# Attention over 6250 keys on one core: output transposes a pair later, values in other rounds, a quarter of the block moves on ScalarE's queue

## The chip, the core and the metric

The kernel runs on one core of a Trainium2 chip. TensorE (PE) multiplies matrices into PSUM, VectorE (DVE), ScalarE (ACT) and GpSimd (POOL) work on SBUF and PSUM, and SyncE (SP) issues DMAs; ACT can issue them too. The engines run side by side and wait for each other by semaphores only. The metric is the device time of one execution in microseconds (us); lower is better.

## The reference, cut to what matters

Eight heads of 64 attend from 512 query rows to 6250 keys and values, then comes a transformer block's rest. `e` is 512, `n` is 6250.

```python
q = (M @ Wq.T).reshape(e, h, dh).transpose(1, 0, 2)
k, v = jnp.split(x @ Wkv.T + bkv, 2, axis=-1)
sim = jnp.einsum('hid,hjd->hij', q, k) * dh ** (-0.5)
sim = jnp.where(mask, sim, -1000000000.0)
out = jnp.einsum('hij,hjd->hid', jax.nn.softmax(sim, axis=-1), v)
out = out.transpose(1, 0, 2).reshape(e, h * dh) @ Wo.T + bo
m = layer_norm(out + M)
z = layer_norm(jax.nn.relu(m @ W1.T + b1) @ W2.T + b2 + m)
```

## The kernel before

The keys are taken in 7 chunks of 896 (first, five in a loop, last), each chunk in 4 pairs of heads p = 0 to 3, each pair in 4 rounds t = 0 to 3, one for 128 query rows. `chunk_schedule` writes one list of steps for a chunk; every engine walks the same list and carries out its part of each step, so the list is the order of work on all queues at once. A step is (letter, pair, index); a pair number below 0 is a pair of the chunk before. The steps:

- **S** (L807, L652): PE computes the scores of the round's two heads into two of three PSUM slots (12 matmuls in float32r, three products for precision); DVE adds the mask, takes the running extreme and writes `prob`. The three slots are a ring, and **K** uses one of them too.
- **E** (L533): ACT takes the exponential of one head's `prob`, with its sum. **X** (L665): DVE transposes 32x32 blocks of both heads of a round from `prob` into `st`. X of round t stands in round t + 1.
- **M** (L366): 16 DMAs on SP's queue carry the blocks of two rounds from `st` to their partitions in `pt`. X of an even round waits until the moves of the same half of `st` one pair earlier have landed.
- **W** (L834): PE multiplies values by the moved probabilities, 7 key tiles of 128 for a pair, into the bank `outT`. W of pair p stands in pair p + 2.
- **C** (L547): ACT copies `outT` to `outT_sb`. **F** (L841): PE transposes that into the bank `tp`. **A** (L672): DVE adds `tp` to the accumulator `acc`.
- **V** (L736 with `tail`, L539): PE projects the values of one key tile into `tp`, ACT copies them to `val`. V and F share the one bank `tp`, so each waits until the one before it has been emptied (`tp_free`). V0 to V3 are made in pair 1, V4 to V6 in pair 2.
- **K** (L736 with `slot`), **H** (L500), **L** (L604): the next pair's keys, their high part on ACT, their low part `k_lo` on DVE. S of the next pair waits for `k_lo`. **Z** (L435 to L446, L554): rescaling of sums and `acc` on POOL, a small exponential on ACT. **Jx**, **Jm**, **J**: loads of `x` and mask, and the split of `x` on POOL. **I**: the loads of `wo`, the residual and the first tiles of `w1` and `w2`, 3 MB in all, in the last chunk.
- After the last chunk: **N** (L675, L678) divides by the sums, **G** (L854) transposes, B and **D** (L551, L681) split the result, **Y** (L770) is the output projection. Then layer norm and the feed-forward loop.

The four rounds of pair 2 of a middle chunk, before:

```
S2.0 E V4 E W0.0 W0.1 W0.2 X1.3 M1.1
S2.1 E V5 E W0.3 W0.4 Z1 X2.0
S2.2 E V6 E W0.5 K3 H3 J X2.1 M2.0
S2.3 E W0.6 C0 E L3 F0 X2.2 A0
```

Of the kernel before, what the change touches and what calls it, by code (L numbers as in the profile page):

```python
# [43 lines left out]
def chunk_schedule(first, last):  # L44

    out = []
    if not first:
        out.append(("M", -1, 1))
    if not last:
        out.append(("Jx", 0, 0))

    def weighted(p, kts):
        return [] if first and p < 0 else [("W", p, kt) for kt in kts]

    for p in range(PAIRS):
        w = p - 2
        keys = not (last and p == PAIRS - 1)
        has_w = not (first and w < 0)

        out.append(("S", p, 0))
        if p == 2:
            out.extend([("E", p, (0, 0)), ("V", 0, 4), ("E", p, (0, 1))])
            out.extend(weighted(w, (0, 1, 2)))
        elif p == 1:  # L70
            out.extend([("E", p, (0, 0)), ("E", p, (0, 1))])
            out.extend(weighted(w, (0, 1, 2)))
            out.append(("V", 0, 0))
        else:
            out.extend([("E", p, (0, 0)), ("E", p, (0, 1))])
            out.extend(weighted(w, (0, 1, 2)))
        if not (first and p == 0):
            out.append(("X", p - 1, 3))
            if p > 0:
                out.append(("M", p - 1, 1))  # L80

        out.append(("S", p, 1))
        if p == 2:
            out.extend([("E", p, (1, 0)), ("V", 0, 5), ("E", p, (1, 1))])
            out.extend(weighted(w, (3, 4)))
        elif p == 1:
            out.extend([("E", p, (1, 0)), ("E", p, (1, 1))])
            out.extend(weighted(w, (3, 4, 5)))
            out.append(("V", 0, 1))
        else:  # L90
            out.extend([("E", p, (1, 0)), ("E", p, (1, 1))])
            out.extend(weighted(w, (3, 4, 5)))
        if not (first and p == 0):
            out.append(("Z", p - 1, 0))
        out.append(("X", p, 0))

        out.append(("S", p, 2))
        if p == 2:
            out.extend([("E", p, (2, 0)), ("V", 0, 6), ("E", p, (2, 1))])
            out.extend(weighted(w, (5,)))  # L100
        else:
            out.extend([("E", p, (2, 0)), ("E", p, (2, 1))])
            out.extend(weighted(w, (6,)))
            if has_w:
                out.append(("C", w, 0))
        if keys:
            out.extend([("K", p + 1, 0), ("H", p + 1, 0)])
        if p == 2 and not last:
            out.append(("J", 0, 0))
        if p == 2 and last:  # L110
            out.append(("I", 0, 0))
        out.extend([("X", p, 1), ("M", p, 0)])
        if p == 0 and not last:
            out.append(("Jm", 0, 0))

        out.append(("S", p, 3))
        out.append(("E", p, (3, 0)))
        if p == 2:
            out.extend(weighted(w, (6,)))
            if has_w:  # L120
                out.append(("C", w, 0))
            out.append(("E", p, (3, 1)))
        elif p == 1:
            out.extend([("V", 0, 2), ("E", p, (3, 1)), ("V", 0, 3)])
        else:
            out.append(("E", p, (3, 1)))
        if keys:
            out.append(("L", p + 1, 0))
        if has_w:
            out.append(("F", w, 0))  # L130
        out.append(("X", p, 2))
        if has_w:
            out.append(("A", w, 0))
            if last and w >= 0:
                out.append(("N", w, 0))
        if last and p == PAIRS - 1:
            out.append(("O", 0, 0))
    if last:
        a, b = PAIRS - 2, PAIRS - 1
        out.extend([("X", b, 3), ("M", b, 1), ("Z", b, 0)])  # L140
        out.extend([("G", 0, 0), ("G", 1, 0), ("B", 0, 0), ("D", 0, 0), ("B", 1, 0), ("D", 1, 0)])
        out.extend([*weighted(a, range(KT)), ("C", a, 0), ("Y", 0, 0), ("F", a, 0), ("A", a, 0), ("N", a, 0)])
        out.extend([("Y", 0, 1), ("Y", 0, 2), ("Y", 0, 3), ("G", a, 0), ("B", a, 0), ("D", a, 0)])
        out.extend([*weighted(b, range(KT)), ("C", b, 0), ("Y", 1, 0), ("F", b, 0), ("A", b, 0), ("N", b, 0)])
# [814 lines left out]
```

## Time and profile before

| what | value |
|---|---|
| three runs | 786.58, 787.69, 788.43 us; median 787.69 |
| the profiled execution | 788.94 us, its span 787.1 us |
| busy share of the span | PE 86%, DVE 74%, ACT 47%, POOL 21% |
| TensorE clock granted, mean | 0.932 of full speed |

The profile comes from one execution. Idle time is put down to what ended it. "Starts" below are us from the start of the span. The setup ends at about 30 us, the seven chunks at about 648, and the output projection and feed-forward part take the rest. S of pair 0 of the fourth chunk starts at 287.17.

### The profile page before, as it was taken

How to read it: one execution, taken by the hardware profiler on the slowest of the kernel's cores; microseconds unless marked ns; L12 is line 12 of the kernel's file. 1: busy time of each engine (PE TensorE's matmuls, PEld its weight loads, DVE VectorE, ACT ScalarE, POOL GpSimd, SP SyncE). 2: the span in 40 equal slices, each digit the busy share in tenths (PEclk: the TensorE clock that was granted, in tenths of full speed). 3: DMA queues.
4: the chain of work that ended last, by engine and by line, in shares of the span. 5: the costliest groups of instructions: out<-in, count | busy, mean ns of one | idle time of the engine just before them, and what ended most of it. 6: DMA issues, size and time to landing. Idle time of an engine off the chain costs nothing.

```text
span 787.1 us, 10971 instructions
## 1 busy us (share of the span) xinstructions
PE 674.7 (86%) x3382; PEld 404.6 (51%) x3382; DVE 581.0 (74%) x715; ACT 367.6 (47%) x658; POOL 163.0 (21%) x239
## 2 busy tenths in 40 slices
PE   4888888899888888898898888888898849699995
PEld 3664444544445444554455444554455425478884
DVE  4498898778887799779987898879878771633333
ACT  4355455554545455555554554555544530333332
POOL 2200320023100420023100320033000070421213
PEclk8889999999999999999999999999999969799998
DMA  8067788767787678868787678867777884022321
GB/s 304 1 155 171 161 181 210 190 157 167 174 237 177 146 179 212 198 140 180 175 237 178 154 175 221 195 142 179 168 170 175 267 192 106 28 80 82 105 80 53
DMA packets 52503, 127.95 MB, mean 163 GB/s; under 512 B 15744, under 2 KB 16256, under 8 KB 52224
## 3 DMA queue, kind: packets, MB, share of 16 engines
q1 hardware_dynamic: 52480, 127.67, 66.5%
q8 instruction: 11, 0.18, 0.1%
q14 instruction: 12, 0.10, 0.0%
HBM read 23.80 MB, written 1.05 MB: 32 GB/s over the span
## 4 chain that ended last, share of the span: by engine, by line
PE 64%; SPq 14%; DVE 10%; issue 6%; DMA 3%; ACT 2%; POOL 0%; DVEq 0%; ACTq 0%; POOLq 0%
PE tail L834 18%; PE slot L807 16%; SPq L366 13%; PE tail L736 10%; PE slot L736 7%; PE slot L887 6%; PE slot L895 5%; DVE st L665 3%; DVE prob L652 3%; DMA pt<-st 2%; DVE k_lo L604 1%; DMA wq_raw<-in_wq 1%; PE tail L841 1%; ACT val L539 1%; DVE stats L689 1%
## 5 line engine op out<-in xcount | busy, mean ns | idle before, releaser
L533 ACT ACTIVATE prob<-prob,negmax 128x896 f32<-128x896 f32 x224 | 234.1, 1045 | 274.7 <-DVE negmax L652 274.7
L652 DVE CUSTOM_DVE_ANT_0 prob<-slot,lower,negmax_old 128x896 f32<-128x896 f32 x224 | 248.8, 1148 | 77.5 <-PE slot L807 73.9
L665 DVE STREAM_TRANSPOSE st<-prob 128x1792 f32<-128x1792 f32 x112 | 228.6, 2041 | 19.8 <-DMA pt<-st 19.3
L834 PE MATMUL tail<-pt,val 128*64 128x512 f32 x784 | 209.4, 664 | 0.4 <-DMA pt<-st 0.4
L807 PE MATMUL slot<-k_hi,q_hi 64*128 64x448 f32 x448 | 98.1, 432 | 50.4 <-DVE k_lo L604 39.5
L834 PEld LDWEIGHTS tail<-pt,val 128*64 128x64 f32 x784 | 54.2, 152 | 110.6 <-issue 110.6
L807 PEld LDWEIGHTS slot<-k_hi,q_hi 64*128 64x128 f32 x448 | 44.0, 191 | 106.1 <-issue 63.4
L807 PE MATMUL slot<-k_hi,q_lo 64*128 64x448 f32 x448 | 88.2, 386 | 0.0
L807 PE MATMUL slot<-k_lo,q_hi 64*128 64x448 f32 x448 | 87.3, 382 | 0.0
L441 POOL TENSOR_TENSOR total<-total,alpha 128x8 f32<-128x8 f32 x28 | 5.8, 206 | 249.8 <-ACT alpha L554 249.8
L807 PEld LDWEIGHTS slot<-k_hi,q_lo 64*128 64x128 f32 x448 | 45.9, 198 | 3.5
L416 POOL TENSOR_SCALAR lower<-mask_raw 128x896 bf16<-128x896 uint8 x28 | 27.2, 971 | 91.5 <-DVE negmax L652 79.7
L807 PEld LDWEIGHTS slot<-k_lo,q_hi 64*128 64x128 f32 x448 | 45.2, 195 | 1.5
L736 PE MATMUL tail<-wv_hi,x_hi 128*128 128x512 f32 x98 | 36.4, 453 | 10.3 <-ACT val L539 10.3
L736 PE MATMUL slot<-x_hi,wk_hi 128*128 128x448 f32 x112 | 36.0, 403 | 8.0 <-DVE x_lo L613 8.0
L533 ACT ACTIVATION_READ_ACCUMULATOR prob<-prob,negmax 128x1 f32 x224 | 42.1, 188 | 0.0
L841 PE MATMUL tail<-ident,outT_sb 128*128 128x128 f32 x112 | 18.7, 291 | 19.6 <-ACT outT_sb L547 14.9
L539 ACT COPY val<-tail 128x512 f32<-128x512 f32 x49 | 28.1, 574 | 15.0 <-PE tail L736 15.0
L736 PEld LDWEIGHTS slot<-x_hi,wk_hi 128*128 128x128 f32 x112 | 19.5, 195 | 30.2 <-issue 29.1
L478 POOL TENSOR_TENSOR hid_lo<-hid,hid_hi 128x512 fp32r<-128x512 f32 x16 | 21.2, 1327 | 66.5 <-DVE hid_hi L720 66.5
L720 DVE CAST hid_hi<-hid 128x512 fp32r<-128x512 f32 x16 | 6.8, 428 | 35.9 <-ACT hid L589 35.8
L435 POOL TENSOR_TENSOR drop<-negmax,negmax_old 128x8 f32<-128x8 f32 x28 | 5.7, 203 | 131.5 <-ACT prob L533 131.0
(107 smaller groups left out, 844.1 us busy)
## 6 DMA issues: line engine op xcount, KB each, us to landing
pt<-st SPq DMA_DIRECT2D x896, 112.0 KB, 2.3
w_raw<-in_w SPq DMA_DIRECT2D x32, 256.0 KB, 2.8
x_raw<-in_x SPq DMA_DIRECT2D x6, 896.0 KB, 5.8
mask_raw<-in_mask SPq DMA_DIRECT2D x7, 448.0 KB, 3.9
mt_raw<-in_mt SPq DMA_DIRECT2D x2, 512.0 KB, 8.0
wq_raw<-in_wq SPq DMA_DIRECT2D x2, 512.0 KB, 8.7
wo_raw<-in_wo SPq DMA_DIRECT2D x1, 1024.0 KB, 4.7
m_res<-in_mn SPq DMA_DIRECT2D x1, 1024.0 KB, 6.9
```

The costliest lines, as they stand in the source:

```text
L366: sp.dma_start(pt[LANES * b:LANES * b + LANES, buf, a], st[LANES * a:LANES * a + LANES, i, b]).then_inc(landed[buf], 16)
L416: nc.gpsimd.tensor_scalar(lower[:, t], mask_raw[:, t], -1.0, -BIG, ALU.add, ALU.mult).then_inc(lower_ready, 1)
L533: nc.scalar.activation(unit, unit, ACT.Exp, bias=negmax[:, p, u:u + 1], scale=-1.0, accum_out=psumrow[:, p, u:u + 1]).then_inc(exp_done, 1)
L539: nc.scalar.copy(val[:, i], tp).then_inc(v_copied, 1)
L652: nc.vector.tensor_tensor_reduce(out=prob[:, i % 2, h].rearrange("p (b n) -> p b n", b=2), in0=slot[:, j, :, :HALF], in1=lower[:, i].rearr ...
L665: nc.vector.transpose(st[:, g].rearrange("p b k (t i) -> p k b t i", t=2)[:, :, :, t2], prob[:, i % 2].rearrange("p h (k b i) -> p (h k) b ...
L736: last = nc.tensor.matmul(dst, stationary(a, k), moving(b, k), start=(n == 0), stop=(n == len(terms) - 1))
L807: last = nc.tensor.matmul(slot[:, j, b, :HALF], q2[qa][rows(h), p, P * i:P * i + P], key_half(p, b, kb)[rows(h)], start=(part == 0), stop= ...
L834: last = nc.tensor.matmul(outT[DH * h:DH * h + DH], val[:, i, head(p, h)], moving, start=(i == 0), stop=(i == KT - 1))
L841: last = nc.tensor.transpose(tp[:, P * t:P * t + P], outT_sb[:, P * t:P * t + P], ident[:])
L887: last = nc.tensor.matmul(slot[:, 2, j], w12[a][:, j, k], mT2[b][:, k], start=(i == 0), stop=(i == len(terms) - 1))
L895: last = nc.tensor.matmul(slot[:, t // 2, t % 2], hid2[a][:, j, P * t:P * t + P], w22[b][:, j], start=first and i == 0, stop=last_one and ...
```

## The change

Three things change in the list of steps; the work itself stays the same.

1. F and A of a pair stand one pair later: C of pair p is in round 2 or 3 of pair p + 2 as before, but F and A are in round 1 of pair p + 3, F ahead of W3, A behind S on DVE. A bank waits for what last stood in it in the list (`bank_plan`), so V5 in pair 2 now waits for A.
2. V1 moves from round 1 to round 2 of pair 1, V5 goes between W3 and W4, V4, V6, V2 and V3 keep their places.
3. M issues 12 of its 16 DMAs on SP; the other 4 are a new step B on ACT's queue, a round later (B0 behind round 3's exponentials, B1 behind round 1's of the next pair).

In the last chunk I stands a round later, behind M2.0; in the ending, G0 goes ahead of W of pair 2 and G1 into it. What B was in the ending is now T.

```diff
+ROUNDS = (
+    ('S E0 E1 W0 W1 W2 X M1 R',
+     'S E0 E1 Z F W3 W4 W5 A X B1',
+     'S E0 E1 W6 C K H X M0 Q',
+     'S E0 E1 L X B0'),
+    ('S E0 E1 W0 W1 W2 V0 X M1',
+     'S E0 E1 Z F W3 W4 W5 A X B1',
+     'S E0 E1 W6 C V1 K H X M0',
+     'S E0 V2 E1 V3 L X B0'),
+    ('S E0 V4 E1 W0 W1 W2 X M1',
+     'S E0 E1 Z F W3 V5 W4 A X B1',
+     'S E0 V6 E1 W5 K H X M0 J',
+     'S E0 W6 C E1 L X B0 I'),
+    ('S E0 E1 W0 W1 W2 X M1',
+     'S E0 E1 Z F W3 W4 W5 A X B1',
+     'S E0 E1 W6 C K H X M0',
+     'S E0 E1 L X B0 O'),
+)
...
+                elif kind in "WC":
+                    step = (kind, p - 2, i)
+                elif kind in "FA":
+                    step = (kind, p - 3, i)
...
+        out.extend([("F", 1, 0), ("A", 1, 0), ("N", 1, 0)])
+        out.extend([("X", b, 3), ("M", b, 1), ("B", b, 1), ("Z", b, 0)])
+        out.extend([("G", 0, 0), ("T", 0, 0), ("D", 0, 0)])
+        out.extend([*(("W", a, kt) for kt in range(3)), ("G", 1, 0), ("T", 1, 0), ("D", 1, 0)])
...
-                        for turn in range(QUAD):
+                        for turn in (0, 1, 2):
                             for a in (0, 2, 1, 3):
...
+                    if kind == "B":
+                        buf = move_buf(p, i)
...
+                        act.wait_ge(xposed, written)
+                        for turn in (3,):
+                            for a in (0, 2, 1, 3):
+                                b = (a + turn) % QUAD
+                                act.dma_start(pt[LANES * b:LANES * b + LANES, buf, a],
+                                              st[LANES * a:LANES * a + LANES, i, b]).then_inc(landed[buf], 16)
...
+            def bank_plan(sched):
+
+                plan, last = {}, None
+                for step in sched:
+                    if step[0] in "VF":
+                        plan[step], last = last, step
+                return plan
```

PE's queue in the loop, pair 2, round 1, from behind the scores of the round to the next round's (`ident` marks F, `wv` marks V, `pt,val` marks two of a W's matmuls). Before:

```order
352 L736 MATMUL tail<-wv_hi,x_hi 128x512 [waits v_copied]
353 L736 MATMUL tail<-wv_hi,x_hi 128x512
354 L736 MATMUL tail<-wv_lo,x_hi 128x512 x2
355 L736 MATMUL tail<-wv_hi,x_lo 128x512 x2
356 L834 MATMUL tail<-pt,val 64x512 [waits v_copied]
357 L834 MATMUL tail<-pt,val 64x512
358 L834 MATMUL tail<-pt,val 64x512 [waits v_copied]
359 L834 MATMUL tail<-pt,val 64x512
360 L807 MATMUL slot<-k_hi,q_hi 128x448 [waits drained2,drained1]
```

And after the change:

```order
351 L821 MATMUL tail<-ident,outT_sb 128x128 [waits outT_copied,v_copied]
352 L821 MATMUL tail<-ident,outT_sb 128x128 x3
353 L814 MATMUL tail<-pt,val 64x512 [waits v_copied]
354 L814 MATMUL tail<-pt,val 64x512
355 L714 MATMUL tail<-wv_hi,x_hi 128x512 [waits acc_added]
356 L714 MATMUL tail<-wv_hi,x_hi 128x512
357 L714 MATMUL tail<-wv_lo,x_hi 128x512 x2
358 L714 MATMUL tail<-wv_hi,x_lo 128x512 x2
359 L814 MATMUL tail<-pt,val 64x512 [waits v_copied]
360 L814 MATMUL tail<-pt,val 64x512
361 L787 MATMUL slot<-k_hi,q_hi 128x448 [waits drained2,drained1]
```

F has come into the round, and V5 waits for `acc_added`, DVE's A, where it waited for a copy of ACT.

DVE's queue of the same round, after the change (L630 is S, L650 is A, L643 is X; before, no A stood between the second S and X):

```order
170 L630 ISA prob,negmax<-slot,lower,negmax_old 128x896 [waits filled2,xposed,zeroed]
171 L630 ISA negmax 128x1
172 L228 REGISTER_ALU
173 L630 ISA prob,negmax<-slot,lower,negmax_old 128x896 [waits filled0,zeroed]
174 L630 ISA negmax 128x1
175 L650 TENSOR_TENSOR acc<-acc,tail 128x512 [waits f_filled,acc_scaled]
176 L642 ISA [waits landed2]
177 L643 STREAM_TRANSPOSE st<-prob 128x14x4x32 [waits exp_done]
```

A stands behind both scores of its round.

ACT's queue from the last exponential of round 0 of pair 0 to the first of round 2, before and after the change:

```order
67 L531 REGISTER_ALU
68 L533 ACTIVATE prob,psumrow<-prob,negmax 128x896 [waits drained0]
69 L554 ACTIVATE alpha<-drop 128x8 [waits drop_ready]
70 L533 ACTIVATE prob,psumrow<-prob,negmax 128x896 [waits drained1]
71 L533 ACTIVATE prob,psumrow<-prob,negmax 128x896 [waits drained2]
```

```order
81 L496 REGISTER_ALU
82 L498 ACTIVATE prob,psumrow<-prob,negmax 128x896 [waits drained0]
83 L532 ACTIVATE alpha<-drop 128x8 [waits drop_ready]
84 L228 ISA
85 L528 DMA pt<-st 32x896 [waits xposed,pv_done,zeroed]
86 L528 DMA pt<-st 32x896 x3
87 L498 ACTIVATE prob,psumrow<-prob,negmax 128x896 [waits drained1]
88 L498 ACTIVATE prob,psumrow<-prob,negmax 128x896 [waits drained2]
```

Four DMAs now stand ahead of the next round's exponentials.

## Rows read from the trace of the kernel before

**Rows 1.** The page's part 4: the chain that ended last, by engine.

```profile
PE 64%; SPq 14%; DVE 10%; issue 6%; DMA 3%; ACT 2%; POOL 0%; DVEq 0%; ACTq 0%; POOLq 0%
```

**Rows 2.** Busy time by stretch: pairs 0 to 3 of the fourth chunk, then three slower pairs.

```profile
core 0: us, PE busy (x) PEld busy (x) DVE busy (x) ACT busy (x) POOL busy (x), PEclk, DMA share, GB/s
287.17:307.18 20.01, 17.07 (x92) 8.92 (x92) 18.33 (x22) 10.32 (x20) 1.82 (x5) 0.91 0.79 176
307.18:332.94 25.76, 23.57 (x116) 13.10 (x116) 20.42 (x23) 12.58 (x24) 2.23 (x7) 0.93 0.88 222
332.94:355.43 22.49, 20.38 (x113) 11.63 (x112) 16.76 (x22) 11.36 (x21) 6.22 (x5) 1.00 0.65 145
355.43:375.45 20.02, 17.08 (x94) 8.94 (x93) 18.13 (x23) 10.70 (x21) 6.47 (x10) 0.91 0.80 180
...
109.30:129.88 20.58, 17.23 (x92) 8.98 (x92) 18.52 (x23) 10.41 (x21) 1.90 (x6) 0.92 0.78 176
178.07:198.60 20.53, 17.15 (x95) 9.00 (x94) 18.10 (x22) 10.65 (x21) 6.42 (x10) 0.92 0.74 166
549.95:570.60 20.65, 17.19 (x92) 9.01 (x92) 18.32 (x22) 10.29 (x20) 1.95 (x6) 0.92 0.75 170
```

**Rows 3.** The chain in order of time, pair 0 into pair 1, two chunks: start, us, what.

```profile
302.25 1.42 PE slot L807 x11
...
306.06 0.01 DVE negmax L652
306.06 1.07 DVE k_lo L604
307.14 0.04 issue
307.18 1.49 PE slot L807 x12
308.68 4.40 PE tail L834 x12
313.08 1.59 PE tail L736 x6
...
397.02 2.73 PE tail L834 x12
```

**Rows 4.** Timeline at pair starts: start, us, engine, line, operation, idle before.

```profile
303.59 0.66 PE L841 MATMUL tail<-ident,outT_sb 128*128 128x128 f32 x4
307.18 0.47 PE L807 MATMUL slot<-k_hi,q_hi 64*128 64x448 f32 x2 [2.94 <-DVE k_lo L604]
...
329.95 0.73 PE L736 MATMUL tail<-wv_hi,x_hi 128*128 128x512 f32 x2 [1.44 <-ACT val L539]
...
332.36 0.66 PE L841 MATMUL tail<-ident,outT_sb 128*128 128x128 f32 x4 [0.75 <-ACT val L539]
...
354.87 0.63 PE L841 MATMUL tail<-ident,outT_sb 128*128 128x128 f32 x4 [2.11 <-ACT outT_sb L547]
```

**Rows 5.** Two starts of pair 1 by stretch, columns as in rows 2.

```profile
395.53:401.20 5.67, 5.67 (x30) 2.86 (x30) 5.39 (x7) 1.72 (x4) 0.40 (x2) 1.00 0.94 284
307.18:312.90 5.72, 5.72 (x24) 2.19 (x24) 5.28 (x7) 1.61 (x4) 0.40 (x2) 0.70 0.96 283
```

**Rows 6.** Timeline of DVE: first score and X of pair 2's round 1; an A.

```profile
340.34 1.15 DVE L652 CUSTOM_DVE_ANT_0 prob<-slot,lower,negmax_old 128x896 f32<-128x896 f32 x1 [1.55 <-PE slot L807]
...
342.49 2.04 DVE L665 STREAM_TRANSPOSE st<-prob 128x1792 f32<-128x1792 f32 x1
...
309.59 0.65 DVE L672 TENSOR_TENSOR acc<-acc,tail 128x512 f32<-128x512 f32 x1
```

**Rows 7.** The moves: duration of one issue, landing, and one M on SP's queue.

```profile
L366 SPq DMA_DIRECT2D pt<-st x896: 507/592/2149, 43.1 to 659.3; - x180
...
DMA to landing us min/median/max: 2.1/2.3/8.7
...
306.75 10.05 SPq L366 DMA_DIRECT2D pt<-st  x16
```

**Rows 8.** X waiting for moves: the total and count; one early, one in the last chunk.

```profile
  DMA pt<-st: 19.3, 22
...
120.04 2.05 DVE L665 STREAM_TRANSPOSE st<-prob 128x1792 f32<-128x1792 f32 x1 [0.98 <-DMA pt<-st]
...
632.51 2.04 DVE L665 STREAM_TRANSPOSE st<-prob 128x1792 f32<-128x1792 f32 x1 [4.16 <-DMA pt<-st]
```

**Rows 9.** The last chunk on SP's queue and PE, and its third wait.

```profile
613.61 0.35 SPq L385 DMA_DIRECT2D wo_raw<-in_wo  x1
...
616.69 33.61 SPq L366 DMA_DIRECT2D pt<-st  x49
...
661.63 6.23 PE L834 MATMUL tail<-pt,val 128*64 128x512 f32 x28 [0.41 <-DMA pt<-st]
```

**Rows 10.** ACT's timeline in round 2 of a pair 0.

```profile
300.31 1.05 ACT L533 ACTIVATE prob<-prob,negmax 128x896 f32<-128x896 f32 x1 [2.21 <-DVE negmax L652]
...
302.42 0.57 ACT L547 COPY outT_sb<-tail 128x512 f32<-128x512 f32 x1
302.89 1.01 ACT L500 ACTIVATE k_hi<-slot,bk_sb 128x896 fp32r<-128x896 f32 x1
```

More of the change, by code:

```diff
@@ L41 @@
 PAIR_LANDED = 16 * QUAD * QUAD
+ROUNDS = (
[16 rows of a table added]
+)
 def chunk_schedule(first, last):
     out = []
[L53 to L59, printed above, removed]
-    for p in range(PAIRS):
[L62 to L137, printed above, removed]
@@ new lines, in chunk_schedule @@
+    for p in range(PAIRS):
+        for t in range(QT):
+            for word in ROUNDS[p][t].split():
+                kind, i = word[0], int(word[1:] or 0)
+                step = (kind, p, i)
+                if kind == "S":
+                    step = (kind, p, t)
+                elif kind == "E":
+                    step = (kind, p, (t, i))
+                elif kind == "X":
+                    step = (kind, p, t - 1) if t else (kind, p - 1, QT - 1)
+                elif kind == "V":
+                    step = (kind, 0, i)
+                elif kind in "WC":
+                    step = (kind, p - 2, i)
+                elif kind in "FA":
+                    step = (kind, p - 3, i)
+                elif kind in "KHL":
+                    step = (kind, p + 1, i)
+                elif kind in "MB":
+                    step = (kind, p - i, i)
+                elif kind == "Z":
+                    step = (kind, p - 1, i)
+                if first and step[1] < 0 or last and (kind in "JRQ" or step[1] == PAIRS) or not last and kind in "IO":
+                    continue
+                out.append(step)
+                if kind == "A" and last and step[1] >= 0:
+                    out.append(("N", step[1], 0))
@@ L138, in chunk_schedule @@
     if last:
         a, b = PAIRS - 2, PAIRS - 1
[L140 to L144, printed above, removed]
@@ L145, in chunk_schedule @@
-        out.extend([("Y", 1, 1), ("Y", 1, 2), ("Y", 1, 3), ("G", b, 0), ("B", b, 0), ("D", b, 0)])
+        out.extend([("F", 1, 0), ("A", 1, 0), ("N", 1, 0)])
+        out.extend([("X", b, 3), ("M", b, 1), ("B", b, 1), ("Z", b, 0)])
+        out.extend([("G", 0, 0), ("T", 0, 0), ("D", 0, 0)])
+        out.extend([*(("W", a, kt) for kt in range(3)), ("G", 1, 0), ("T", 1, 0), ("D", 1, 0)])
+        out.extend([*(("W", a, kt) for kt in range(3, KT)), ("C", a, 0), ("Y", 0, 0), ("F", a, 0), ("A", a, 0), ("N", a, 0)])
@@ L146, in chunk_schedule @@
+        out.extend([("Y", 0, 1), ("Y", 0, 2), ("Y", 0, 3), ("G", a, 0), ("T", a, 0), ("D", a, 0)])
+        out.extend([*(("W", b, kt) for kt in range(KT)), ("C", b, 0), ("Y", 1, 0), ("F", b, 0), ("A", b, 0), ("N", b, 0)])
+        out.extend([("Y", 1, 1), ("Y", 1, 2), ("Y", 1, 3), ("G", b, 0), ("T", b, 0), ("D", b, 0)])
         out.extend([("Y", 2, t) for t in range(QT)])
@@ L837, in body @@
                     if kind == "F":
-                        tp_free(c, kind, p, i)
+                        tp_free(c, banks[step])
                         pe.wait_ge(outT_copied, n + 1)
@@ L845, in body @@
                         if p == 0:
-                            for h in range(2):
-                                j, before = unit_use(c, PAIRS - 1, QT - 1, h)
-                                pe.wait_ge(drained[j], before + 1)
-                            j, before = unit_use(c, PAIRS - 1, 1, 1)
-                            pe.wait_ge(drained[j], before + 1)
+                            emptied = dict(unit_use(c, PAIRS - 1, t, h) for t in range(QT) for h in range(2))
+                            for j in range(RING):
+                                pe.wait_ge(drained[j], emptied[j] + 1)
                         if p >= 2:
```

41 lines of the change are left out of this document (20 added, 21 removed).

## The prediction

> **What bounds the kernel now.** I read the chain that ended last first: PE holds 64% of it, SP's queue 14% [rows 1]. So the chunks decide, and I cut the fourth one at the starts of its pairs [rows 2]: pair 0 takes 20.01 us, pair 1 25.76, pair 2 22.49, pair 3 20.02, together 88.3. The difference is V: four in pair 1, three in pair 2.
>
> In pairs 0 and 3 DVE is busy 18.1 to 18.3 of 20 us, which looks like the bound. It isn't. From 287.17 to the end of F, PE has no idle time; then it idles 2.94 us for `k_lo` [rows 3, 4]. The loop that closes is: PE does S, W, S, W, S, W, K, S; DVE takes the last scores and `k_lo`; PE may start the next pair. From the end of the last scores at 303.70 to 307.18 that hand-over is 3.48 us [rows 3]. F (0.66 us) lies inside it and costs nothing today. Anything added on PE ahead of the last S lengthens the pair.
>
> After the hand-over the granted clock drops: W0 to W2 take 4.40 us [rows 3], and the stretch shows 0.70 of full speed, so part of it is at 1.2 GHz. In the one pair 1 where it stayed at 2.4 (1.00 in [rows 5]) the same three W took 2.73 us [rows 3], 1.67 less, and I take 1.65 as the price of one drop. This happens at nearly every start of pairs 0, 1 and 3, hence the 0.91 of both 20 us pairs against 1.00 in pair 2 [rows 2].
>
> SP's queue is the other candidate. An M takes 10.05 us for 16 DMAs [rows 7], two per pair are 20.1 us, as much as the pair itself. X waits for moves 19.3 us in 22 places [rows 8]. Yet where the wait is half a us, PE is ahead of or level with it, and pairs with no such effect still take 20.0. It shows in the slower pairs only, 20.53 to 20.65 us [rows 2].
>
> **The change, part by part.**
>
> *F in round 1, pairs 0 and 3.* PE executes F (0.62 us net, four transposes) between S1 and W3, with nothing waited for: its input was copied a pair ago. It leaves the hand-over, where it was free, and enters the path ahead of the last S. Such a pair goes from 20.0 to 20.65. There are 12 of them ahead of the last pair; 8 of about 20.0 lose 0.63 each, 5.0 us; the four at 20.5 to 20.65, which SP's queue held, lose about 0.1 each. Sum **+5.4**. If F were hidden there too, it would be 0; if also the four lose the whole, 7.5.
>
> *Pairs 1 and 2.* I take them from S of pair 1 to S of pair 3, 48.25 us now (355.43 - 307.18). In pair 1, F at the end waits 0.75 us for V3's copy and then runs; in round 1 it waits for V0's copy, which ACT makes while PE does S1 (1.42 us). So the 0.75 goes: 25.76 becomes 25.0. The 1.44 us wait of V3 stays [rows 4]. V1 in round 2 instead of round 1 is the same work on the same path and costs nothing: K, 2.67 us, lies between it and V2, over ACT's copy of V1.
>
> In pair 2, count PE from its first S: S 1.43, V4 1.6, W 2.73, S 1.43, F 0.62, W3 0.91, so V5 could start at 8.7. It waits for A. DVE can take the round's scores only when PE has finished them (7.2); now it is just so, DVE idles 1.55 us before them, and X follows 2.15 us after they start [rows 6]. A comes between: scores to 9.4, A 0.58, so V5 starts at 10.1. That is a **new wait of 1.35 us** for PE, and W4, S, V6, W5, K stand behind it. The rest is V5 1.6, W4 0.95, S 1.43, V6 1.6, W5 1.0, K 2.67, S 1.43, ending at 20.8. The old F waited 2.11 us for C [rows 4]; that wait goes, but PE then waits for `k_lo` instead, 3.48 us after its last S: the pair ends at 24.3, against 22.49. What was late by C was only 0.3 us later than `k_lo`. The two pairs come to 49.3, or +1.03; six times (the first chunk has no F there) **+6.2**. If A came with no wait, it would be 6 x (1.03 - 1.35) = -1.9; if ACT makes V5's copy late for V6 as well, another 0.5 each, +9.
>
> *First chunk.* No F in its pair 2: **-0.2**.
>
> *Twelve DMAs on SP, four on ACT.* At 0.63 us a DMA an M takes 7.6 us on SP. X gets its buffer about 2.5 us earlier, which ends the waits of [rows 8]; what that is worth in the body is already in the 0.1 above, since PE's path is next. On ACT there is no such row. The nearest is SP's own, 0.59 us an issue [rows 7], four are 2.5 us. Bounds: near 0 if ACT's compute goes on meanwhile, 5.1 us if each issue waits for one of SP's. At 2.5, B1 fills ACT's idle time between round 1's and round 2's exponentials, 2.21 us in such a pair, and holds round 2 up by some 0.2 us; the exponentials, C and `k_hi` behind it end at 303.9 [rows 10], 2 us ahead of L at 306.06 [rows 3]. So it costs 0. B0 lies in the hand-over, where nothing of ACT is awaited.
>
> What could undo this is weighed apart. The rows show only SP's 0.59 us an issue [rows 7]. The Trainium skill, Perfetto Trace Analysis, DMA Instruction - HWDGE (DVE, Sync), says that the descriptor generator is one block that an issuing sequencer locks for itself; by that, issues from SP and ACT come one after the other. This is the second rival below. The skill's DMA: Bandwidth & Descriptors, Issuing engines are not separate DMA queues, says that issuing from several engines saves the issuing time only; by that the gain is SP's 2.5 us a move and no more, and no run here shows it.
>
> *Last chunk and ending.* Today the 3 MB of loads go out at 613.61, ahead of M2.0, whose X then waits 4.16 us [rows 8, 9]. After, they go behind M2.0 (which waits for W6 till 616 anyway): that 4.16 goes, but M2.1 meets the loads. Its X stood at 641.96; M2.1 now starts at 627 behind the loads, as M2.0 did at 616.69, and that one landed 15.8 us later. With 4 fewer on the queue I get 640 to 642. The ending gains further: G0 and three W come ahead of N1, M3.1 lands 2.5 us earlier and the wait of 0.41 [rows 9] goes, while B3.1 holds ACT's T by some 2 us. Counted through, W of pair 3 starts 2 to 4.6 us earlier. I take **-3.0**, bounds -6 and 0.
>
> *Clock.* Each drop costs 1.65 us. Before, PE idled 2.94 us behind F at pairs 0 and 1; after, 3.5 us with no F. At pair 3 it idled 2.1, did F, then S; after, 2.4 and S. The former speaks for drops as before, the latter for a few less. I take two of nineteen fewer, **-3.0**; bounds +2 and -13.
>
> Sum: 5.4 + 6.2 - 0.2 - 3.0 - 3.0 = +5.4. The profiled execution is 788.94 us, 1.25 above the median, about one drop of the clock. I set the sum on the median: 787.69 + 5.4 = **793 us**.
>
> **The rivals.**
>
> 1. *The clock stays up (faster).* Pairs 0 and 3 without a drop would fall to 19.0, for DVE needs 18.1 to 18.3. If eight more of nineteen starts stay at 2.4 GHz, 8 x 1.65 = 13 us less: **780**. For it: with 12 DMAs SP's queue no longer caps a pair at 20.1, so a start without a drop pays in full. Against: only about one start in nineteen was spared, and the idle time before pairs 0 and 1 grows.
> 2. *The issues collide.* Four DMAs then hold ACT 5.1 us. In round 2 of pairs 0 and 3 the exponentials, C and `k_hi` shift by 2.7 us and `k_lo` by about 0.55: 12 x 0.55 = 6.6. In pair 1 V2 waits 0.7 us for V1's copy: 6 x 0.7 = 4.2. Time 793 + 10.8 = **804**. It decides from an issue of more than about 1.1 us on ACT.
> 3. *SP's queue was the bound (faster).* Then pairs 0 and 3 go to DVE's 18.3 plus little, 18.8, instead of 20.65: 12 x 1.85 = 22 less, **771**. Against: PE's unbroken work from 287.17.
> 4. *A wash.* The ending gains its full 6 and A is half hidden: 793 - 3 - 4 = **786 to 788**.
>
> **How the numbers follow.** Forecast (787 to 799 by its bounds) 0.52; rival 1 0.17; rival 2 0.12; rival 3 0.06; rival 4 0.13. The range reaches rivals 1 and 2, 779 to 804, leaving out rival 3 and the ends of the others. 0.2% is 1.6 us, about what a measurement of this kernel tells from no change. Slower by more than that: 0.48 of the forecast and rival 2, 0.60. Same: 0.04 of the forecast and most of rival 4, 0.14. Faster: rivals 1, 3 and the rest, 0.26.
>
> **What would show it.** In the trace after: pairs 0 and 3 at 20.6 us with PE unbroken from the first S to the last and idle 3.5 us for `k_lo`; V in round 1 of pair 2 with 1.3 us of idle put down to DVE's `acc`; F waiting for nothing; pair 1 at 25.0 and pair 2 at 24.3; an M of 7.6 us on SP; an issue on ACT of about 0.6 us; X hardly waiting for moves; the wait of 4.16 gone. Wrong if the clock column of pairs 0 and 3 rises well above 0.91, if V5 doesn't wait, or if issues on either queue take over 1 us.

## The result: 793.43 us after 787.69, and the profile after

The changed kernel takes **793.43 us** (median of 5 runs, 791.33 to 794.77) against 787.69 before: ratio 1.0069, 95% interval 1.0047 to 1.0090. It is slower, by 5.7 us. In a later series it was 1.0090 (1.0061 to 1.0118). The profiled execution took 793.74 us, its span is 791.9 us (before 787.1).

Busy shares and queues, from the page of the kernel after (engine, us, share of the span, instructions; then queue, packets, MB, share of 16 engines):

```profile
PE 664.3 (84%) x3382; PEld 402.3 (51%) x3382; DVE 580.6 (73%) x715; ACT 367.9 (46%) x658; POOL 162.7 (21%) x239
q1 hardware_dynamic: 41728, 101.97, 49.8%
q10 hardware_dynamic: 10752, 25.70, 13.2%
```

q10 is ScalarE's queue with its quarter of the moves. No engine is nearer to full than before.

From here on I cut the time at the starts of `k_lo` on VectorE, because they are easy to find in every kernel of this study. One such interval is a pair: from the `k_lo` that ends pair 0 to the one that ends pair 1, and so on. The fourth chunk after, pairs 1, 2, 3 and then pair 0 of the fifth chunk (columns as in [rows 2]; the one with 0.xx or 1.00 behind POOL is the granted clock):

```profile
307.68:331.15 23.47, 21.54 (x110) 12.69 (x110) 18.41 (x25) 11.48 (x23) 1.84 (x5) 0.93 0.79 192
331.15:356.81 25.66, 22.18 (x116) 12.59 (x116) 18.41 (x25) 12.42 (x25) 5.25 (x7) 1.00 0.52 122
356.81:375.80 18.99, 15.46 (x92) 8.53 (x92) 18.41 (x25) 10.81 (x22) 6.89 (x9) 1.00 0.86 204
375.80:396.34 20.54, 17.02 (x92) 9.33 (x92) 18.41 (x25) 10.31 (x21) 2.76 (x6) 0.92 0.83 222
```

The same four intervals of the kernel before, cut in the same way:

```profile
305.98:329.24 23.26, 21.33 (x106) 11.63 (x106) 18.47 (x23) 11.50 (x23) 1.83 (x5) 0.93 0.89 226
329.24:354.07 24.83, 22.06 (x116) 12.67 (x116) 18.50 (x25) 12.27 (x25) 5.25 (x7) 1.00 0.66 148
354.07:374.25 20.18, 17.65 (x96) 9.37 (x96) 18.29 (x25) 10.86 (x22) 6.90 (x9) 0.92 0.80 181
374.25:394.33 20.08, 17.14 (x92) 8.92 (x92) 18.34 (x25) 10.31 (x21) 2.76 (x6) 0.92 0.78 175
```

Pair 1 is 0.21 longer, pair 2 0.83 and pair 0 0.46. Pair 3 is 1.19 us *shorter*, and its clock column differs: 1.00 where it was 0.92, with TensorE busy 15.46 us instead of 17.65.

Who waited for whom after (total us, times, longest):

```profile
PE slot L787 <- DVE k_lo L582: 63.7, 20, 3.8
PE tail L714 <- ACT val L504: 10.2, 7, 1.6
PE tail L714 <- DVE acc L650: 8.8, 6, 1.5
DVE st L643 <- DMA pt<-st: 7.0, 1, 7.0
PE tail L814 <- DMA pt<-st: 5.9, 1, 5.9
```

The two of TensorE that the change made or lengthened, in order of time (start, us, what, idle time before it):

```profile
308.88 0.66 PE L787 MATMUL slot<-k_hi,q_hi 64*128 64x448 f32 x2 [3.52 <-DVE k_lo L582]
343.70 0.73 PE L714 MATMUL tail<-wv_hi,x_hi 128*128 128x512 f32 x2 [1.46 <-DVE acc L650]
```

The first S of a pair waits 3.52 us for `k_lo`, where it waited 2.94 behind F [rows 4]. Pair 3's first S, which came behind F before, now waits for `k_lo` too. V5 waits 1.46 us for the addition A, six times, which is new. The transposes wait for moves once, 7.0 us, instead of 19.3 us in 22 places [rows 8]. V3 still waits for V2's copy.

### The profile page after: what moved, and what is told of

Read it like the earlier page. It is cut to its first block and busy times, and to the rows that moved or that the text cites. A ratio compares the mean times of both kernels' runs of the same rounds, so it can differ in the third digit from the quotient of the medians.

```text
span 791.9 us, 11082 instructions
## 1 busy us (share of the span) xinstructions
PE 664.3 (84%) x3382; PEld 402.3 (51%) x3382; DVE 580.6 (73%) x715; ACT 367.9 (46%) x658; POOL 162.7 (21%) x239
## 5 line engine op out<-in xcount | busy, mean ns | idle before, releaser
L630 DVE CUSTOM_DVE_ANT_0 prob<-slot,lower,negmax_old 128x896 f32<-128x896 f32 x224 | 249.0, 1149 | 103.5 <-PE slot L787 98.7
L643 DVE STREAM_TRANSPOSE st<-prob 128x1792 f32<-128x1792 f32 x112 | 228.3, 2039 | 7.0 <-DMA pt<-st 7.0
L814 PE MATMUL tail<-pt,val 128*64 128x512 f32 x784 | 202.6, 641 | 5.9 <-DMA pt<-st 5.9
L814 PEld LDWEIGHTS tail<-pt,val 128*64 128x64 f32 x784 | 51.3, 146 | 102.9 <-issue 102.9
L714 PE MATMUL tail<-wv_hi,x_hi 128*128 128x512 f32 x98 | 36.4, 453 | 19.0 <-ACT val L504 10.2
L714 PEld LDWEIGHTS tail<-wv_hi,x_hi 128*128 128x128 f32 x98 | 14.8, 190 | 45.3 <-issue 17.6
L465 ACT ACTIVATE k_hi<-slot,bk_sb 128x896 fp32r<-128x896 f32 x28 | 28.2, 1007 | 11.3 <-PE slot L714 11.3
```

The source lines that it names most:

```text
L465: nc.scalar.activation(kst[0][:, p % 2].rearrange("p (b n) -> p b n", b=2), slot[:, 0, :, :HALF], ACT.Identity, bias=bk_sb[:, p:p + 1]).th ...
L630: nc.vector.tensor_tensor_reduce(out=prob[:, i % 2, h].rearrange("p (b n) -> p b n", b=2), in0=slot[:, j, :, :HALF], in1=lower[:, i].rearr ...
L643: nc.vector.transpose(st[:, g].rearrange("p b k (t i) -> p k b t i", t=2)[:, :, :, t2], prob[:, i % 2].rearrange("p h (k b i) -> p (h k) b ...
L714: last = nc.tensor.matmul(dst, stationary(a, k), moving(b, k), start=(n == 0), stop=(n == len(terms) - 1))
L814: last = nc.tensor.matmul(outT[DH * h:DH * h + DH], val[:, i, head(p, h)], moving, start=(i == 0), stop=(i == KT - 1))
```

## The experiments

All of them are edits of the table that orders the steps, or of who issues the moves. In its rounds R and Q load the next chunk's `x` and mask, and O is POOL's split of `wo` in the last chunk; no experiment moves these three. Each ratio is to runs of the kernel before on the same chip (its median there was 786.3 to 787.2).

### Undoing the parts: F back, all moves on SP, moves on ScalarE alone

`f_back` puts F and A back where they were and keeps the other two parts. `F1` is F of the pair before last's values, `p - 2`, as `F` in round 1 is that of `p - 3`. The edit in all four pairs is like this one in pair 0 (against the changed kernel):

```diff
-     'S E0 E1 Z F W3 W4 W5 A X B1',
+     'S E0 E1 Z W3 W4 W5 X B1',
...
-     'S E0 E1 L X B0'),
+     'S E0 E1 L F1 X A1 B0'),
```

> The changed kernel with F and the addition back where they were, in round 3 of the pair that makes them; values spread and moves on ScalarE's queue stay. Theory: F leaves the path in eight pairs (8 x 0.63 = 5.0 us less) and V5's wait goes (6 x 1.46 = 8.8 less); back come F behind V3 (6 x 0.75 = 4.5 more) and F's wait ahead of pair 3 (6 x 0.2 = 1.2 more): 793.4 - 8.1 = 785.3 us (782 to 789), with up to 6 us more where the four starts of pair 3 at full clock are lost. Rival (the time was lost by the moves on ScalarE's queue or by the values, not by F): 791 to 795 us.

Measured: **781.52 us**, ratio 0.9934 (0.9912 to 0.9955), 5 to 6 us faster than before and 11 to 12 faster than the changed kernel. The theory had 785.3 (782 to 789), the rival 791 to 795. It came out half a us below the theory's range, and the gain is nearly half as much again as the 8.1 forecast, but the cause is the theory's: the loss of the change is F's move. Pairs 1, 2 and 3 of its fourth chunk:

```profile
303.26:326.19 22.93, 20.99 (x106) 11.77 (x106) 18.30 (x25) 11.48 (x23) 1.83 (x5) 0.93 0.88 209
326.19:351.15 24.96, 22.19 (x116) 12.54 (x116) 18.49 (x25) 12.29 (x25) 5.25 (x7) 1.00 0.52 125
351.15:371.23 20.08, 17.60 (x96) 9.58 (x96) 18.36 (x23) 10.80 (x22) 6.88 (x9) 0.92 0.84 197
```

Against the changed kernel pair 1 is 0.54 and pair 2 0.70 shorter, and pair 3 is back at clock 0.92 and 20.08.

`act_alone` is the kernel before with the third part only; Bm issues the four moves of turn 3 on ScalarE's queue, a round after SP's twelve:

```diff
+            out.append(("Bm", p - 1, 1))
...
+        out.append(("Bm", p, 0))
...
-                        for turn in range(QUAD):
+                        for turn in (0, 1, 2):
```

> The kernel before with only the third part of the change: four of the sixteen moves issued on ScalarE's queue, a round after SP's twelve. Theory: SP's queue was no bound, the transposes' waits for moves (19 us in 22 waits) go but lay beside TensorE; what is gained is the few starts at full clock: 785 us (782 to 788), against 787.7 before. Rival 1 (SP was the bound): about 771 us. Rival 2 (issues in front of exp delay the scores' way through): 793 to 797 us.

Measured: **782.89 us**, ratio 0.9946 (0.9927 to 0.9965). So the third part is worth 4 us. It is not the 17 of the rival in which SP's queue was the bound, and there is no loss. In its profile the four pairs of 20.48 to 20.74 us before are 2.7 us shorter in all, and one more start was spared its fall of the clock, 1.5 us. Parts 2 and 3 and the new order of the ending together (`f_back`) are at 0.9934, so the spread values are worth nothing beyond the error.

`sp_all` is the changed kernel with `for turn in range(QUAD)` on SP and without ScalarE's block:

> The changed kernel with all sixteen moves of a tile pair on SP, none on ScalarE's queue. Theory: moves cost SP 10 us again beside a pair of 19 to 20.5 us, the transposes wait for moves 20 to 30 times, and the pairs that ran in 19.0 us go back to 20 to 20.6: 797 us (793 to 801). Rival (ScalarE's issues stand in front of its exp and cost more than they free): faster than the changed kernel, 786 to 790 us.

Measured: **798.59 us**, ratio 1.0171 (1.0128 to 1.0214), as the theory said. Its pairs 2 and 3:

```profile
329.42:355.11 25.69, 22.21 (x116) 12.58 (x116) 18.41 (x23) 12.41 (x25) 5.25 (x7) 1.00 0.64 144
355.11:374.31 19.20, 15.44 (x92) 8.55 (x92) 18.50 (x23) 10.86 (x22) 6.88 (x9) 1.00 0.81 180
```

The miss is in a detail: pair 3 did not go back to 20 us, it still ran at clock 1.00, in 19.20 instead of 18.99. The moves do not decide whether the clock falls there. They cost 0.2 us in such a pair; the waits for moves are back (19.5 us in 23 places), and the last two pairs before the ending take 50.17 instead of 49.19. Its six executions range from 796 to 807 us, so the size of its loss is less certain than most here.

### Is V5's wait worth its length? v5_first, v5_half, and the changed kernel again

`v5_first` takes V5 out from behind A:

```diff
-     'S E0 E1 Z F W3 V5 W4 A X B1',
+     'S E0 V5 E1 Z W3 W4 F X A B1',
```

> The changed kernel with one round of pair 2 written otherwise: V5 stands right behind S again, and F and its addition come after W4 and the transpose of the prob tile, so that V5 no longer stands behind the addition. Theory (what stands on the path of TensorE costs its own time): the wait of V5 for VectorE's addition, 1.46 us in each of six chunks, goes, and nothing takes its place: 793.4 - 8.8 = 784.7 us (783 to 787). Rival (the next S was late anyway, the wait is cover): the idle time turns up at the next start of S, 792 to 794 us. Both: pairs 0 and 3 unchanged, 20.5 and 19.0 to 20.6 us.

Measured: **789.73 us**, ratio 1.0034 (1.0016 to 1.0052). It lies between the theory (783 to 787) and the rival (792 to 794): 3 to 4 us gained instead of 8.8. The wait is gone and pair 2 is 1.7 us shorter, but pair 3 lost its clock:

```profile
328.35:352.28 23.93, 21.94 (x116) 12.68 (x116) 18.38 (x23) 12.26 (x25) 5.25 (x7) 1.00 0.54 131
352.28:372.85 20.57, 17.04 (x92) 9.09 (x92) 18.41 (x23) 10.81 (x22) 6.90 (x9) 0.92 0.82 193
```

`v5_half` fills only part of the wait, with W4:

```diff
-     'S E0 E1 Z F W3 V5 W4 A X B1',
+     'S E0 E1 Z F W3 W4 V5 A X B1',
```

> The changed kernel with W4 ahead of V5 instead of behind it, so that half a microsecond of the 1.46 us for which V5 waits is filled with W4. Theory (each wait filled is worth its length, and pair 3 ran at full clock after a long enough wait in pair 2): pair 2 goes from 25.65 to 25.15 us, 6 x 0.5 = 3.0 us less, if pair 3 keeps its 18.99 us in most chunks: about 790; where pair 3 goes back to 20.6 us as in v5_first, the refund is gone and it is 793 to 796 us, slower than the changed kernel though it waits less. Rival (the clock of pair 3 has nothing to do with V5's wait): some pairs 3 at 19.0 in this kernel and some not, no order in it.

Measured: **792.26 us**, ratio 1.0069 (1.0042 to 1.0095). V5 waits 3.6 us in all instead of 8.8. Pair 2 and pair 3:

```profile
328.26:352.90 24.64, 22.02 (x116) 12.67 (x116) 18.41 (x23) 12.41 (x25) 5.26 (x7) 1.00 0.54 127
352.90:373.20 20.30, 16.77 (x92) 9.42 (x92) 18.40 (x23) 10.80 (x22) 6.85 (x9) 0.92 0.83 196
```

Pair 2 gained 1.03 us, six times; pair 3 gave back 1.3, four times. The kernel waits less and is, within the error, no faster. That is the case that the expectation put at 793 to 796; it came out a little below it.

`after_again` is the changed kernel, unchanged, with these:

> The changed kernel once more, on the same chip and beside the same runs of before as the two below. Theory (V5's wait leaves pair 3 a clock that does not fall): again four or more of six pairs 3 at 19.0 us, ratio to before 1.005 to 1.009, 791 to 794 us. Rival (chance): fewer, and the ratio up to 1.015.

Measured: **793.49 us**, ratio 1.0090 (1.0061 to 1.0118). Its pairs 3 took 21.98, 20.43, 18.99, 18.96, 18.99, 18.98; in the first profile they took 22.05, 20.44, 18.99, 18.99, 18.98, 18.98. In the later series the same four are spared. A chance falling of the clock does not do that. Over the six chunks whose pair 3 has a pair 0 behind it, the count of pairs 3 at 1.00 is 4, 4 and 5 with the full wait of V5 (changed kernel, again, `sp_all`), and 0 and 0 without it or with part of it (`v5_first`, `v5_half`; also 0 in `w_handover` below). It is a strong tilt and not a switch: `f_back`, `act_alone` and `loads_later`, without that wait, have one each. The first chunk has no F ahead of its V5 and so no wait there, and its pair 3 is spared in none of the profiles of the changed kernel (both), `sp_all`, `v5_first` and `v5_half`: of the five pairs 3 that do follow a full wait, 4, 4 and 5 ran at 1.00.

These counts are from one profiled execution each, but the mean clock of every execution goes the same way: 0.942 to 0.951 in the eleven of the changed kernel, 0.930 to 0.940 in the twelve of `v5_first`, 0.930 to 0.935 in the six of `v5_half`.

### How full is the hand-over? w_handover

`v5_first`, and in pairs 0 and 3 W6 and C go behind the last S:

```diff
-     'S E0 E1 W6 C K H X M0 Q',
-     'S E0 E1 L X B0'),
+     'S E0 E1 K H X M0 Q',
+     'S E0 W6 C E1 L X B0'),
```

> Kernel v5_first with W6 and its copy C moved, in pairs 0 and 3, from round 2 to behind the last S, where TensorE waits 3.5 us for k_lo. Theory (the hand-over is empty time): W6 leaves the path, 0.45 to 0.5 us in each of 14 pairs: 789.7 - 6.5 = 783 us (781 to 786), pairs 0 and 3 20.55 -> 20.1. Rival (the hand-over starts when K and its copies are done, so S comes no earlier; or the moves that wait for W6 hold up the transposes): 789 to 793 us.

Measured: **779.80 us**, ratio 0.9912 (0.9893 to 0.9931), 9.6 us below `v5_first` by the ratios. It gains more than the theory's 783 (781 to 786). Its mechanism holds: pairs 3 and 0 went from 20.57 and 20.56 to 19.97 and 20.00, and three clock drops went as well (one pair 1 at 21.98, two pairs 0 at 18.93), which the theory had not counted on.

```profile
347.56:367.53 19.97, 17.09 (x92) 9.31 (x92) 18.41 (x25) 10.33 (x21) 6.88 (x9) 0.91 0.78 187
```

TensorE does the same work here as in the 20.57 of `v5_first` (17.09 against 17.04). Only its place changed. This is the mirror of what F's move did.

### Shortening the hand-over: klo_early, klo_03, klo_fill, k_first

`k_lo` needs the `slot` that K filled in round 2 and `k_hi`, and not the last scores. `klo_early` is `f_back` with L ahead of the last scores on VectorE, and `k_hi` (H) ahead of C on ScalarE, in all pairs but the H of pair 2 (pair 0, against `f_back`):

```diff
-     'S E0 E1 W6 C K H X M0 Q',
-     'S E0 E1 L F1 X A1 B0'),
+     'S E0 E1 W6 K H C X M0 Q',
+     'L S E0 E1 F1 X A1 B0'),
```

> Kernel f_back with VectorE's k_lo taken ahead of the last scores of each pair instead of behind them, and the copy k_hi ahead of the copy outT_sb on ScalarE. Theory (the hand-over of 3.5 us is two scores and k_lo in a row on VectorE): S of the next pair starts after the first of the two scores; pairs 0 and 3 lose 1.2 us, 13 or 14 times, pair 1 loses nothing (V3 stands there), pair 2 nothing (F waits for outT_sb there): 781.5 - 16 = 766 us (762 to 772). Rival (VectorE, 18.6 us of work per pair, gives it back: k_lo in front only makes the scores later, and the next rounds of S wait for drained slots): 776 to 783 us.

Measured: **787.09 us** (12 executions, 780.27 to 793.73, a far wider spread than the others), ratio 0.9980 (0.9955 to 1.0004). It is 4 to 6 us slower than `f_back`, slower even than the rival's 776 to 783, and not for the rival's reason. Pairs 1, 2, 3 and 0:

```profile
305.09:326.03 20.94, 19.32 (x110) 11.49 (x109) 18.38 (x23) 11.24 (x22) 1.83 (x5) 1.00 0.99 244
326.03:354.18 28.15, 24.32 (x116) 14.46 (x114) 18.50 (x22) 12.73 (x24) 2.67 (x6) 0.88 0.56 131
354.18:375.81 21.63, 18.26 (x100) 9.79 (x96) 18.45 (x23) 10.36 (x20) 9.44 (x10) 0.92 0.71 170
375.81:394.50 18.69, 16.96 (x92) 9.43 (x92) 18.28 (x22) 10.29 (x20) 2.75 (x6) 0.91 0.78 190
```

and V3, with what it waited for:

```profile
329.94 0.74 PE L713 MATMUL tail<-wv_hi,x_hi 128*128 128x512 f32 x2 [3.08 <-ACT val L503]
```

Pair 0 fell to 18.69, with VectorE busy 18.28 of it. That pair is now VectorE's. But V3 waits 3.08 us instead of 1.44: the copy of V2 stands behind an exp, the exp behind the last scores, and those now behind `k_lo`. Pair 2 shows a clock of 0.88 where it was never below 1.00; pair 1 is at 1.00 where it was at 0.93, so the fall seems to have moved (`k_lo`, at which the rows are cut, stands earlier too; the two pairs together take 49.09 us against 47.89 in `f_back`).

`klo_03` keeps L early in pairs 0 and 3 only:

> Kernel klo_early with the early k_lo in pairs 0 and 3 alone; pairs 1 and 2 as in f_back. Theory (klo_early failed in pairs 1 and 2, where k_lo in front of the scores holds up ScalarE's exp, and with it the copies val and outT_sb for which V3 and F wait: pair 2 took 28.1 us against 24.95): pairs 3 and 0 lose 1.3 us each against f_back, pairs 1 and 2 stay at 23.0 and 24.95: 781.5 - 16 = 766 us (763 to 770). Rival (the clock falls longer once the hand-over is shorter, as the 0.88 of klo_early's pair 2): 775 to 785 us.

Measured: **769.17 us**, ratio 0.9770 (0.9738 to 0.9801). The theory holds; the failure of `klo_early` was pairs 1 and 2. V3's longer waits for copies are 6.5 us of it (16.7 against 10.2 in all); what else makes up the 18 us between the two kernels I did not take apart. `klo_fill` mends those pairs instead, by work put into their waits. Against `klo_early`, rounds 2 and 3 of pair 1, then rounds 1 to 3 of pair 2:

```diff
-     'S E0 E1 W6 V1 K H C X M0',
-     'L S E0 V2 E1 V3 F1 X A1 B0'),
+     'S E0 E1 V1 K H X M0',
+     'L S E0 V2 E1 W6 C V3 X B0'),
...
-     'S E0 E1 Z W3 V5 W4 X B1',
-     'S E0 V6 E1 W5 K H X M0 J',
-     'L S E0 W6 C E1 F1 X A1 B0 I'),
+     'S E0 V5 E1 Z W3 W4 F X A B1',
+     'S E0 V6 E1 W5 W6 K H C X M0 J',
+     'L S E0 E1 F1 X A1 B0 I'),
```

> Kernel klo_early, and W6 of pair 1 between V2 and V3 (where TensorE waits 1.44 us for ScalarE's copy), F of that pair behind V5 in the next pair's round 1, W6 of pair 2 in round 2 so that F waits for nothing. Theory: 0.5 to 1.4 us less in pairs 1 and 2 each, six chunks: 6 to 14 us below klo_early. Rival (pairs 1 and 2 are held by the sum on TensorE and the order does not matter, or the moves that wait for W6 come late): within 2 us of klo_early.

Measured: **767.80 us**, ratio 0.9766 (0.9744 to 0.9789), 17 to 19 us below `klo_early`, more than the 6 to 14 expected. What stands out in its waits is one line, VectorE for `k_hi`:

```profile
DVE k_lo L581 <- ACT k_hi L464: 36.6, 23, 3.5
```

K needs a slot that round 1 empties, so it may stand first. `k_first` against `klo_fill`, in pair 3 (pair 0 is the same with a Q behind it), then pair 1, then pair 2:

```diff
-     'S E0 E1 W6 K H C X M0',
+     'S K E0 H E1 W6 C X M0',
...
-     'S E0 E1 V1 K H X M0',
-     'L S E0 V2 E1 W6 C V3 X B0'),
+     'S K E0 H E1 V1 X M0',
+     'S E0 V2 E1 W6 C V3 L X B0'),
...
-     'S E0 V6 E1 W5 W6 K H C X M0 J',
+     'S K E0 H V6 E1 W5 W6 C X M0 J',
```

> Kernel klo_fill with K right behind S in round 2 of every pair and k_hi between the two exp, and k_lo of pair 1 back behind the last scores. Theory (VectorE waited 36.6 us in 23 waits for k_hi, and V3 1.3 us for the copy of V2, that stood behind a late exp): pairs 0 and 3 stay at 18.7, pairs 1 and 2 lose 1.3 us and up to 1.5 us in six chunks: 767.8 - 12 = 756 us (752 to 762). Rival (VectorE's 18.6 us a pair and TensorE's sum are what is left, the waits lie beside them; or S of the next pair now waits for the late k_lo): 765 to 772 us.

Measured: **745.35 us**, ratio 0.9470 (0.9435 to 0.9505). This is faster than both kernels by over 5%, and below the theory's range of 752 to 762. Its fourth chunk, pairs 1, 2, 3 and 0:

```profile
283.41:304.83 21.42, 20.41 (x118) 12.12 (x114) 20.39 (x26) 12.43 (x25) 1.84 (x5) 1.00 0.89 234
304.83:324.08 19.25, 18.88 (x100) 11.50 (x100) 16.16 (x20) 10.37 (x22) 1.90 (x6) 1.00 0.78 191
324.08:344.94 20.86, 18.73 (x112) 10.11 (x108) 18.35 (x23) 11.01 (x21) 10.25 (x10) 1.00 0.69 167
344.94:363.42 18.48, 16.75 (x92) 9.55 (x92) 18.22 (x23) 11.10 (x21) 2.75 (x6) 0.91 0.84 202
```

and its busy shares:

```profile
PE 653.5 (88%) x3382; PEld 403.4 (55%) x3382; DVE 577.9 (78%) x715; ACT 367.0 (50%) x658; POOL 162.9 (22%) x239
```

(`k_lo` stands elsewhere in pair 1, so the cut between the first two is shifted.) The four come to 80.0 us against 88.7 in the changed kernel. VectorE no longer waits for `k_hi` long enough to be listed. TensorE is busy in 98% of the second interval and VectorE in 99% of the fourth. The clock stands at 1.00 in three of the four. How much of the 9 us a chunk is order and how much clock I did not take apart.

### The ending: loads_later

`f_back` with the last chunk's loads (I) moved from pair 2's last round to pair 3's first:

```diff
-     'S E0 W6 C E1 L F1 X A1 B0 I'),
+     'S E0 W6 C E1 L F1 X A1 B0'),
-    ('S E0 E1 W0 W1 W2 X M1',
+    ('S E0 E1 W0 W1 W2 X M1 I',
```

> Kernel f_back with the weight loads of the last chunk issued a round later, behind M2.1 instead of behind M2.0. Theory (the 6.5 us wait of the transpose and the 5.9 us wait of W for moves in the last pair come from loads that share the DMA engines with M2.1): both waits halve or go, and the end comes 2 to 4 us earlier: 778.5 us (777 to 781). Rival (the last rounds are set by the chain of W, C, Y and alpha whatever the moves do): 781 to 782 us.

Measured: **784.00 us**, ratio 0.9959 (0.9939 to 0.9978), above both the theory (777 to 781) and the rival (781 to 782), and not faster than `f_back` (0.9934). The wait of the transpose is gone (6.5 us in `f_back`, no line here), and another took its place, in a list of who waited for whom:

```profile
PE slot L747 <- DVE ao_lo L658: 8.7, 2, 7.1
```

From the last start of `k_lo` to the end it is 169.8 us, against 168.3 in `f_back`. The new wait comes from the edit itself. From the chain that ended last (start, us, what):

```profile
629.02 5.37 DMA wo_raw<-in_wo
634.45 1.89 POOL wo_hi L431
636.42 4.87 POOL wo_lo L433
641.29 4.45 POOL m_res L436
...
648.30 0.76 PE slot L747
```

`wo` lands at 634.4, some 7 us later than POOL had used it in `f_back` (627.44), POOL's steps on it and on the residual (O) end at 645.7, and only behind them come the last Z and the output projection. So this run trades one wait for another. It shows neither that the waits for moves set the end nor that they don't.

## Why the prediction came out as it did, step by step

**What bounds the kernel: right.** TensorE's unbroken work from the first S to the last, and then the hand-over, set a pair. `w_handover`, `klo_03` and `f_back` all show it from another side.

**F in round 1 of pairs 0 and 3: right in mechanism, the price too high.** Where the clock fell as before, pair 0 went from 20.02 to 20.55, and pair 3 from 20.12 to 20.58 in `v5_first`, which has F in the same place there: 0.46 to 0.53 us a pair, against the 0.63 forecast. The four pairs that SP's queue had held (20.48 to 20.74 before) did not lose 0.1 each but gained it, since F's half a us and about 2 us of relief in all outweigh each other there. The term that the forecast put at 5.4 came to 12 x 0.46 - 2.0 = 3.5. TensorE idles 3.52 us behind the last S, against 3.5 forecast.

**Pairs 1 and 2: right in mechanism, a little low.** From the first S of pair 1 to the first S of pair 3 it is 358.01 - 308.88 = 49.13 us, against 49.3. V5 waits 1.46 us for `acc`, against 1.35. In the `k_lo` cut the sum of both is longer by 1.04 to 1.30 us in five of the six chunks from the second on (in the fifth by 2.8, since the kernel before had its spared start there), together 8.75, of which some 1.6 is clock: 7.1 against 6.2.

**First chunk: mis-sized.** Forecast -0.2; by the time of its first `k_lo` after the weights the changed kernel is 1.6 us ahead (43.65 against 45.26) with 0.1 more in pairs 1 and 2. The experiments, whose work ahead of that point is the same or nearly so, have it anywhere from 41.80 to 46.91, so I count this as no effect of the change. It stands in the sum of the two profiles all the same.

**Twelve and four moves: right.** An M takes 7.60 us on SP, an issue on ScalarE 0.62, both as forecast, and no line shows an exp that waits for them. The relief of 2.0 us above is what the forecast had in its F term, 4 x 0.53 = 2.1.

**Last chunk and ending: the term that failed.** Forecast -3.0; from the last start of `k_lo` to the end:

```profile
617.31:787.10 169.79, 142.68 (x612) 101.17 (x612) 77.85 (x117) 53.85 (x90) 49.06 (x57) 0.91 0.37 107
```

before, and after:

```profile
622.89:791.90 169.01, 140.00 (x612) 99.10 (x612) 78.45 (x117) 53.64 (x90) 49.07 (x57) 0.91 0.39 112
```

That is -0.8. The step "M2.1 meets the loads, I get 640 to 642" failed. In order of time after, from the loads to the last pair (start, us, what):

```profile
621.66 7.60 SPq L331 DMA_DIRECT2D pt<-st  x12
...
629.37 0.51 SPq L350 DMA_DIRECT2D wo_raw<-in_wo  x1
...
632.68 30.52 SPq L331 DMA_DIRECT2D pt<-st  x36
...
649.79 2.04 DVE L643 STREAM_TRANSPOSE st<-prob 128x1792 f32<-128x1792 f32 x1 [6.98 <-DMA pt<-st]
```

The last pair starts 5.4 us later than before (first S at 624.09 against 618.66), so the 640 to 642 of the forecast are 645.4 to 647.4 here. M2.1 starts as forecast, 8.6 us behind that S. But its last move lands 17.1 us after its start, at 649.77, where the forecast's numbers give 13 to 15. The transpose behind it comes 2.4 to 4.4 us later than forecast, and the wait of 4.16 us [rows 8] turned into one of 6.98 in a later round. The chain that ended last runs through it, and then through ScalarE's four issues of B3.1, 2.7 us that stand ahead of `alpha` (the forecast had "some 2 us"):

```profile
640.16 9.61 DMA pt<-st
...
657.45 0.62 ACTq L528
...
658.11 0.10 ACT alpha L532
```

W of pair 3 starts 42.9 us behind the last pair's first S, as before (43.0), and not 2 to 4.6 us earlier. What the wait alone is worth stays open, since `loads_later` took it away and paid with later loads.

**Clock: right in the sum, wrong in the make-up.** Forecast -3.0. The measured pieces: four pairs 3 spared, 4 x 1.58 = -6.3; the spared pair 1 of before lost, +1.6; pair 3 of the first chunk at a clock of 0.85 for a longer time, +1.45 beyond F; together -3.3. The forecast looked for spared starts at pair 3, where they came, but because of the idle time right ahead of it. That is 2.51 us in the changed kernel where the clock stayed up, 2.51 where it fell (pair 3 of the second chunk), and 2.49 and 2.52 in `v5_first` and `v5_half`, which spared none: it is not what decides. The runs tie it to V5's wait: with it most pairs 3 are spared, without it one of six at most. So part of what the forecast charged to V5's wait was paid back, as far as these runs tell by the very wait, and the forecast had no step for that. In `v5_first` it cost the gain.

The terms measured are 3.5 + 7.1 - 1.7 - 0.8 - 3.3 = +4.8, and the spans differ by 4.8 us, as they must, for the terms are read from those two profiles without a gap. Against the forecast they are off by -1.9, +0.9, -1.5, +2.2 and -0.3. That these nearly cancel, and the sum of +5.4 lies so close to the +5.7 of the medians, is luck; what was foreseen is that F in a full round and V5's new wait make the kernel slower, and by how much within 2 us each.

**The rivals.** The clock staying up came true in four pairs, one other was lost, and the rival needed eight; it was outweighed. Issues that collide: no. In this stretch both queues issue (ACT's exp in the second row):

```profile
304.90 7.73 SPq L331 DMA_DIRECT2D pt<-st  x12
307.79 1.04 ACT L498 ACTIVATE prob<-prob,negmax 128x896 f32<-128x896 f32 x1
307.96 1.17 ACTq L528 DMA_DIRECT2D pt<-st  x2
309.16 1.26 ACTq L528 DMA_DIRECT2D pt<-st  x2
```

SP issues twelve from 304.90 to 312.6 at 0.64 us each while ScalarE issues four at 0.58 to 0.63 each, and the exp of 307.79 takes its usual 1.04. The Trainium skill, Perfetto Trace Analysis, DMA Instruction - HWDGE (DVE, Sync), says that an issuing sequencer locks the descriptor generator. How much of an issue the lock covers it doesn't say; if it covered most of one, the issues here would have taken about twice as long. The trace does not show that, and the measurement decides. SP's queue as the bound: no, `act_alone` gained 4 us and not 17. A wash: no.

## What to carry to other kernels

Before moving work off a late place, look whether the engine is idle there: F was free in a hand-over of 3.5 us and cost 0.5 us in each pair once it stood in a full round, and putting W6 into that same gap brought the time back. Then ask what the hand-over itself consists of; here `k_lo` stood behind scores that it doesn't need, and K behind products that don't need it, and writing them in the order in which they are wanted, with work put into the waits that this made, took 5% off. And try a reordering in each kind of pair apart: the same edit gained 12 us in pairs 0 and 3 and lost more than that in pairs 1 and 2, in part because there another copy stood behind the scores.
